# Starting the attention jobs 13 instead of 16 ticks behind the first feed-forward job, and the second feed-forward jobs 22 instead of 25

## The chip, the core and the metric

The kernel runs on one core of a Trainium2 chip. The metric is the device time of one execution, in microseconds (us). The core's engines are called PE (TensorE, matrix products and transposes), DVE (VectorE), ACT (ScalarE), POOL (GpSimd) and SP (SyncE, which issues the DMAs); each runs its own instructions in order and waits for the others by semaphores.

## What is computed

Sixteen sequences of 512 tokens with 128 channels go through four residual parts, all in fp32. `_L0_attn_a_ref` is an RWKV model of four layers (64 layer-and-sequence steps), `_L0_ffn_ref` a gated feed-forward with blockwise FP4 rounding of its inputs, `_L0_attn_b_ref` a causal attention with one head.

```python
    x = L0_attn_a_x
    x = x + _L0_attn_a_ref(_layernorm(x, axis=-1), ...)
    x = x + _L0_ffn_ref(_layernorm(x, axis=-1), L0_ffn_w_gate, L0_ffn_w_up, L0_ffn_w_down)
    x = x + _L0_attn_b_ref(_layernorm(x, axis=-1), L0_attn_b_w_qkv, L0_attn_b_w_out, L0_attn_b_b_out)
    x = x + _L0_ffn_ref(_layernorm(x, axis=-1), L0_ffn_w_gate, L0_ffn_w_up, L0_ffn_w_down)
    return x
```

## The kernel before

All sixteen sequences stay in SBUF as `X[0]` to `X[15]`, each 128 partitions by 512. The kernel is a software pipeline over **ticks**. Each engine has a loop `for t in range(TICKS)` (DVE L532, POOL L723, ACT L983, PE L1267) that calls the same small functions in a fixed order every tick; each call stands a fixed number of ticks behind the start of its job, and does nothing when no job is at that stage. Nothing in the program lets one tick wait for another: the engines drift against each other as far as the semaphores between them allow.

There are four kinds of jobs, one per sequence: the 64 RWKV steps (one per tick from tick 0), 16 first FFN jobs from tick `FFN_AT` = 69, 16 attention jobs from tick `ATT_AT` = 85, and 16 second FFN jobs from tick `FFN2_AT` = 94. `ffn_job(t)` and `att_job(t)` give the job that starts at tick t, or None.

An FFN job that starts at tick s occupies the engines so. DVE takes the statistics of the input, `f_bn` (two instructions of L225), at s-1. ACT normalises (`f_z`, four of L754) at s+2, keeps the turned input (`keep_fx`) at s+4, and takes silu of the four gate products (`silu`, L903) at s+5. PE turns the input (`f_turn`, L1037) at s+5, makes gate and up products (`f_gate` L1185 and `f_up` L1192) for token chunk 0 at s+5 and for chunks 1 to 3 at s+6, turns the quantised hidden values (`h_turn`, three groups of L1201) at s+8, and multiplies down (`down`, L1213) at s+9, after which ACT writes the new `X` (`keep_x`, L938).

An attention job that starts at tick s: statistics on DVE (`a_bn`, two of L225) at s+2, `a_rsqrt` on POOL at s+5, `a_z` on ACT (L754) at s+3, `a_turn` on PE (L1037) at s+4, `a_keys` (L1229) at s+5, `a_values` (L1237) and the four `similarity` products (L1245) at s+6 with `a_mask`, `a_max` on DVE and `a_exp` on ACT (L973), then `p_turn` (L1253), `keep_pt` (L980), `p_values` (L1263) and `a_add` (DVE L526) at s+7. The second FFN job of the same sequence takes its statistics at s+8.

PSUM has eight banks, and all of them are shared. `hand_over` fixes, in the order of PE's program, whom a bank's next writer waits for. Banks `bF0` and `bF1` carry the FFN's gate and up products of chunks 1 and 3 (`bG`, `bU`) and the attention's similarities 0, 1 and 3 (`bS`); `bR` and `bKV` carry the FFN's rounding (`pM`) and similarity 2 and `p_values`.

```python
        bX, pX, bG, pG, bU, pU = bK, pK, [bV, bF0], [pV, pF0], [bO, bF1], [pO, pF1]
        bS, pS, bY, pY = [bF0, bF1, bR, bF0], [pF0, pF1, pR, pF0], [bT, bO, bT, bO], [pT, pO, pT, pO]
```

ACT evaluates its functions from a table that holds one set at a time. Exp (of `a_exp`) and silu are in different sets, and the compiler puts an ACT_TABLE_LOAD wherever the set changes.

Of the kernel before, what the change touches and what calls it, by code (L numbers as in the profile page):

```python
# [31 lines left out]
FFN_AT = NR + 5  # L32
LN2_LAG = 6
EARLY = 10
ATT_AT, FFN2_AT = FFN_AT + 16, FFN_AT + 25
TICKS = FFN2_AT + 35


# [1340 lines left out]
```

## Time and profile before

| | |
|---|---|
| time, median of 3 runs | 1372.84 us (1369.95 to 1373.4) |
| span of the profiled execution, first to last instruction | 1368.5 us |
| PE busy | 1303.0 us (95%) |
| ACT busy | 1257.6 us (92%) |
| DVE busy | 1238.3 us (90%) |
| POOL busy | 1122.6 us (82%) |
| the 16 DMA engines | 4.2% for the data queue |

Busy time is the time in which an engine had at least one instruction in it. The profiled execution's own time is its span and what lies around it; the median of the runs stands 4.3 us above the span. PE's records are modelled at their ends, so a row of PE is best read by the distance from its start to the start of the next one.

### The profile page before, as it was taken

How to read it: one execution, taken by the hardware profiler on the slowest of the kernel's cores; microseconds unless marked ns; L12 is line 12 of the kernel's file. 1: busy time of each engine (PE TensorE's matmuls, PEld its weight loads, DVE VectorE, ACT ScalarE, POOL GpSimd, SP SyncE). 2: the span in 40 equal slices, each digit the busy share in tenths (PEclk: the TensorE clock that was granted, in tenths of full speed). 3: DMA queues.
4: the chain of work that ended last, by engine and by line, in shares of the span. 5: the costliest groups of instructions: out<-in, count | busy, mean ns of one | idle time of the engine just before them, and what ended most of it. 6: DMA issues, size and time to landing. Idle time of an engine off the chain costs nothing.

```text
span 1368.5 us, 23485 instructions
## 1 busy us (share of the span) xinstructions
PE 1303.0 (95%) x7285; PEld 935.9 (68%) x7285; DVE 1238.3 (90%) x2169; ACT 1257.6 (92%) x2539; POOL 1122.6 (82%) x1216
## 2 busy tenths in 40 slices
PE   3799999999999999999999999988999998899997
PEld 1356677667766677667766677766777876677776
DVE  6999999999999999999999999569999577978994
ACT  6899999999999999999999999877887899998884
POOL 6888998888888888888899999979998465666784
PEclk9899999999999999999999999999999999999999
DMA  7000000000000000000000000010000000000011
GB/s 237 1 1 1 1 1 1 1 21 13 1 0 2 1 1 1 1 1 1 1 1 1 8 24 21 27 32 1 1 1 1 2 1 1 1 16 16 24 32 39
DMA packets 26923, 18.54 MB, mean 14 GB/s; under 512 B 1072, under 2 KB 26160, under 8 KB 26800
## 3 DMA queue, kind: packets, MB, share of 16 engines
q1 hardware_dynamic: 26800, 17.05, 4.2%
q8 instruction: 59, 0.97, 0.3%
q14 instruction: 64, 0.52, 0.1%
HBM read 12.85 MB, written 4.19 MB: 12 GB/s over the span
## 4 chain that ended last, share of the span: by engine, by line
PE 67%; ACT 11%; DVE 9%; POOL 6%; issue 5%; DMA 0%; SPq 0%; DVEq 0%; ACTq 0%; POOLq 0%
PE ps L1154 12%; PE ps L1137 12%; PE ps L1213 5%; PE ps L1037 4%; PE ps L1192 4%; PE ps L1185 4%; PE ps L1144 3%; PE ps L1124 3%; PE ps L1089 3%; PE ps L1090 3%; PE ps L1102 3%; PE ps L1082 3%; PE ps L1263 3%; PE ps L1201 2%; PE ps L1245 2%
## 5 line engine op out<-in xcount | busy, mean ns | idle before, releaser
L1137 PE MATMUL ps<-xk,W 128*128 128x512 f32 x512 | 250.7, 593 | 1.4 <-ACT kf L864 1.4
L1154 PE MATMUL ps<-W,kf 128*128 128x128 f32 x2048 | 249.6, 275 | 0.0
L754 ACT ACTIVATE z<-X,ln_rs 128x128 f32<-128x128 f32 x512 | 239.7, 720 | 3.7 <-POOL ln_rs L603 3.7
L1154 PEld LDWEIGHTS ps<-W,kf 128*128 128x128 f32 x2048 | 239.2, 192 | 2.3 <-issue 1.0
L864 ACT ACTIVATE kf<-ps 128x512 f32<-128x512 f32 x256 | 186.6, 817 | 0.5 <-PE ps L1137 0.5
L871 ACT ACTIVATE kf<-kf 128x1024 f32<-128x1024 f32 x128 | 164.6, 1286 | 0.0
L1037 PEld LDWEIGHTS ps<-idn,z 128*128 128x128 f32 x664 | 83.1, 143 | 113.3 <-issue 87.3
L1137 PEld LDWEIGHTS ps<-xk,W 128*128 128x128 f32 x512 | 91.9, 190 | 92.1 <-issue 89.0
L710 POOL TENSOR_TENSOR W<-W,hsc 128x704 f32<-128x704 f32 x64 | 88.8, 1388 | 59.0 <-DVE W L493 58.8
L1037 PE MATMUL ps<-idn,z 128*128 128x128 f32 x664 | 102.0, 277 | 29.8 <-ACT z L754 20.7
L601 POOL TENSOR_TENSOR ln_rs<-ln_rs,mhalf 128x8 f32<-128x8 f32 (+1 forms) x70 | 127.9, 1827 | 0.0
L1185 PE MATMUL ps<-WG,d 128*128 128x352 f32 x256 | 98.5, 468 | 6.3 <-ACT er L903 5.4
L652 POOL TENSOR_TENSOR rv<-rv,aa 128x512 f32<-128x512 f32 x64 | 81.7, 1276 | 25.6 <-DVE aa L365 25.3
L670 POOL TENSOR_TENSOR dh<-h 128x512 f32<-128x512 f32 x64 | 66.5, 1039 | 43.3 <-ACT h L857 43.3
L225 DVE BATCH_NORM_STATS2 ln_st<-X 128x6 f32<-128x256 f32 x256 | 96.7, 419 | 0.1
L704 POOL TENSOR_TENSOR W<-W,hsc 128x704 f32<-128x704 f32 x64 | 88.8, 1389 | 8.6 <-DVE hsc L481 8.6
L1192 PE MATMUL ps<-WU,d 128*128 128x352 f32 x256 | 93.8, 466 | 1.9 <-DVE W L462 1.4
L1124 PEld LDWEIGHTS ps<-W,rc 128*128 128x128 f32 x512 | 68.0, 194 | 31.6 <-issue 29.0
L675 POOL TENSOR_TENSOR X<-X,cr 128x512 f32<-128x512 f32 x64 | 81.9, 1279 | 4.9 <-DVE cr L417 4.9
L657 POOL TENSOR_TENSOR er<-er,rc 128x512 f32<-128x512 f32 x64 | 81.6, 1276 | 0.0
L646 POOL TENSOR_TENSOR er<-er,bb 128x512 f32<-128x512 f32 x64 | 81.5, 1274 | 0.0
L663 POOL TENSOR_TENSOR p<-p,rc 128x512 f32<-128x512 f32 x64 | 81.5, 1273 | 0.0
(176 smaller groups left out, 3962.5 us busy)
## 6 DMA issues: line engine op xcount, KB each, us to landing
X<-x_in SPq DMA_DIRECT2D x16, 256.0 KB, 6.9
xi<-x_in SPq DMA_DIRECT2D x16, 256.0 KB, 2.9
out<-X SPq DMA_DIRECT2D x16, 256.0 KB, 2.3
W<-weights SPq DMA_DIRECT2D x4, 832.0 KB, 8.4
W<-fp4w SPq DMA_DIRECT2D x1, 560.0 KB, 3.8
row<-rows SPq DMA_DIRECT2D x1, 192.0 KB, 2.9
wqkv<-qkv SPq DMA_DIRECT2D x1, 96.0 KB, 5.7
idn<-ident SPq DMA_DIRECT2D x1, 64.0 KB, 3.1
```

Source lines behind the costliest of these rows:

```text
L225: last = e.bn_stats(g.of(g.st, n)[:, 2 * k:2 * k + 2, :].rearrange("p a s -> p (a s)"), src[:, k * 256:(k + 1) * 256].rearrange("p (a c) - ...
L601: e.tensor_tensor(rs[:, 0, :], rs[:, 2, :], mhalf[:, 0:k], ALU.pow).then_inc(*own.next())
L704: e.tensor_tensor(h, h, spread(hsc[n % 2][:, 0, k * 44:(k + 1) * 44], 44), ALU.mult).then_inc(fh_y[k], 1)
L754: last = e.activation(chunk(dst, j), chunk(src, j), ACT.Identity, bias=rs[:, 1, j:j + 1], scale=rs[:, 0, j:j + 1])
L864: e.activation(kf[r % 3][:, f, :], (pF0, pF1)[f % 2][:, :], ACT.Relu).then_inc(relu_done[f], 1)
L871: e.activation(both, both, ACT.Square).then_inc(sq_done[k], 1)
L1037: last = e.transpose(chunk(dst, j), chunk(src, j), idn[:, :])
L1124: last = e.matmul(chunk(pO, j), chunk(rc[r % 2], j), w_of(r, WO), start=True, stop=True)
L1137: e.matmul((pF0, pF1)[f % 2][:, :], w_of(r, WCK + f), xk[r % 2][:, :], start=True, stop=True).then_inc(kf_mm[f], 1)
L1154: last = e.matmul(chunk(pKV, j), kf[r % 3][:, f, j * 128:(j + 1) * 128], w_of(r, WCV + f), start=f == 0 and j == 0, stop=f == 3, skip_grou ...
L1185: e.matmul(pG[j % 2][:, 0:I], chunk(fx[n % 2], j), WG[:, :], start=True, stop=True).then_inc(g_mm, 1)
L1192: e.matmul(pU[j % 2][:, 0:I], chunk(fx[n % 2], j), WU[:, :], start=True, stop=True).then_inc(u_mm, 1)
```

## The change

Two numbers in one line: the first attention job starts at tick 82 instead of 85, the first job of the second FFN at tick 91 instead of 94. The distance between these two stays 9 ticks, the first FFN and the RWKV part keep their ticks. `TICKS` follows `FFN2_AT` and falls from 129 to 126.

```diff
 FFN_AT = NR + 5
 LN2_LAG = 6
 EARLY = 10
-ATT_AT, FFN2_AT = FFN_AT + 16, FFN_AT + 25
+ATT_AT, FFN2_AT = FFN_AT + 13, FFN_AT + 22
 TICKS = FFN2_AT + 35
```

The same compute instructions are issued, in another order on PE, DVE, ACT and POOL; SP's order is the same. ACT has 20 table loads before and 24 after.

On ACT, the place where the first attention job takes its exponentials (`a_exp`, L973, out `kf`), with the FFN's silu on L903 and its Abs on L916. Before:

```order
L938 ACTIVATE X<-ps 128x512
L973 ACT_TABLE_LOAD
L973 ACTIVATE kf,sm<-ps,sm 128x128
L965 ACTIVATE sr<-ps 128x512
L958 ACTIVATE ag<-ps 128x512
L973 ACTIVATE kf,sm<-ps,sm 128x256
L973 ACTIVATE kf,sm<-ps,sm 128x384
L952 ACTIVATE xc<-ps 128x512
L926 ACTIVATE W<-ps 96x512
L973 ACTIVATE kf,sm<-ps,sm 128x512
L933 ACTIVATE ps<-X 128x512
L754 ACTIVATE z<-X,at_rs 128x128 x4
```

And the same place in the program of the change:

```order
L973 ACT_TABLE_LOAD
L973 ACTIVATE kf,sm<-ps,sm 128x128
L965 ACTIVATE sr<-ps 128x512
L958 ACTIVATE ag<-ps 128x512
L973 ACTIVATE kf,sm<-ps,sm 128x256
L973 ACTIVATE kf,sm<-ps,sm 128x384
L952 ACTIVATE xc<-ps 128x512
L926 ACTIVATE ed<-ps 96x512
L973 ACTIVATE kf,sm<-ps,sm 128x512
L903 ACT_TABLE_LOAD
L903 ACTIVATE er<-ps 128x352
L916 ACTIVATE ps<-W 128x2x352
```

Before, the last silu of the first FFN lies behind ACT when the first exponential comes. Now the first attention job's exponentials stand between silus of the first FFN, so the table is loaded back behind them; this happens in two ticks (88 and 89), with two loads in each.

On PE, the place around the first attention job's `p_values` (L1263). Before, the tick held beside it only the last of the first FFN's turns and down products (L1201, L1213):

```order
L1245 MATMUL ps<-xc,ag 128x512
L1037 MATMUL ps<-idn,z 128x128 x4
L1201 MATMUL ps<-idn,W 96x128 x4
L1263 MATMUL ps<-sr,kf 128x128 x10
L1245 MATMUL ps<-xc,ag 128x128
L1213 MATMUL ps<-WD,ed 128x128 x12
L1253 MATMUL ps<-idn,big 128x128 x7
```

And now it stands among gate and up products (L1185, L1192) too:

```order
L1245 MATMUL ps<-xc,ag 128x512
L1037 MATMUL ps<-idn,z 128x128 x4
L1201 MATMUL ps<-idn,W 96x128 x4
L1192 MATMUL ps<-WU,d 128x352
L1263 MATMUL ps<-sr,kf 128x128 x10
L1185 MATMUL ps<-WG,d 128x352
L1192 MATMUL ps<-WU,d 128x352
L1185 MATMUL ps<-WG,d 128x352 x2
L1192 MATMUL ps<-WU,d 128x352 x2
L1201 MATMUL ps<-idn,W 128x128 x8
```

The job whose p_values stand there is the same; it is the FFN work around it that is of an earlier stage, by three ticks.

On DVE, the place where the first attention statistics (`a_bn`, at_st) come: in the program of the change they stand in a tick in which every stage of the first FFN on DVE but `f_bn` is still full.

```order
 L462 TENSOR_TENSOR W<-er,ps 128x352
 L255 TENSOR_REDUCE xsc<-z 128x32
+L225 BN_STATS at_st<-X 128x6 x2
 L446 SCALAR_TENSOR_TENSOR z<-ps,z 128x512
 L462 TENSOR_TENSOR W<-er,ps 128x352
```

Two instructions came into this tick (84), and into the next two; before, the first three of them stood in ticks 87 to 89.

## Rows read from the trace of the kernel before

**Rows 1.** The page: busy time of the engines, and slices of DVE and granted clock.

```profile
PE 1303.0 (95%) x7285; PEld 935.9 (68%) x7285; DVE 1238.3 (90%) x2169; ACT 1257.6 (92%) x2539; POOL 1122.6 (82%) x1216
...
DVE  6999999999999999999999999569999577978994
...
PEclk9899999999999999999999999999999999999999
```

**Rows 2.** Busy time by stretch, cut at PE's tick ends, ticks 84 to 98.

```profile
core 0: us, PE busy (x) PEld busy (x) DVE busy (x) ACT busy (x) POOL busy (x), PEclk, DMA share, GB/s
993.00:1002.90 9.90, 9.60 (x57) 7.16 (x56) 9.90 (x19) 8.15 (x18) 9.11 (x11) 1.00 0.01 2
1002.90:1039.80 36.90, 36.90 (x225) 28.86 (x224) 36.79 (x64) 30.61 (x62) 32.37 (x32) 1.00 0.00 1
1039.80:1049.40 9.60, 9.60 (x62) 7.76 (x61) 9.00 (x15) 8.00 (x18) 7.68 (x9) 1.00 0.00 1
1049.40:1059.20 9.80, 9.11 (x55) 6.85 (x53) 9.05 (x16) 7.20 (x16) 7.92 (x10) 1.00 0.00 0
1059.20:1069.10 9.90, 8.54 (x59) 6.98 (x58) 6.19 (x12) 9.60 (x22) 8.13 (x9) 1.00 0.01 2
1069.10:1082.00 12.90, 12.41 (x91) 10.54 (x90) 4.76 (x14) 11.15 (x30) 3.90 (x8) 1.00 0.01 2
1082.00:1092.40 10.40, 10.40 (x79) 8.98 (x78) 5.60 (x17) 7.68 (x22) 2.39 (x6) 1.00 0.00 0
1092.40:1131.80 39.40, 39.08 (x263) 31.03 (x262) 31.46 (x94) 37.36 (x108) 24.89 (x46) 1.00 0.01 1
```

**Rows 3.** PE's instructions in order of time, in tick 91: start, length, releaser.

```profile
1060.59 1.06 PE L1201 MATMUL ps<-idn,W 128*128 128x128 f32 x8 [1.36 <-POOL W L710]
1061.49 0.39 PE L1245 MATMUL ps<-xc,ag 128*128 128x128 f32 x2
1061.71 2.84 PE L1213 MATMUL ps<-WD,ed 128*128 128x128 f32 x24
1064.39 1.06 PE L1237 MATMUL ps<-AW,xc 128*128 128x128 f32 x8
...
1068.08 0.60 PE L1037 MATMUL ps<-idn,z 128*128 128x128 f32 x4
```

**Rows 4.** DVE's busy time in its ticks 83 and 84, and the attention's statistics.

```profile
993.10:1003.00 9.90, 9.90 (x20) 1.00 0.01 2
1003.00:1012.30 9.30, 9.30 (x18) 1.00 0.00 0
...
L225 DVE BATCH_NORM_STATS2 at_st<-X x32: 400/416/428, 1031.8 to 1191.0; 128x6 f32<-128x256 f32 x32
```

**Rows 5.** Busy time by stretch, as rows 2, in PE's ticks 99 and 103.

```profile
1131.80:1144.80 13.00, 10.02 (x61) 7.46 (x60) 8.89 (x23) 12.18 (x29) 6.71 (x12) 1.00 0.00 1
...
1191.70:1209.60 17.90, 17.40 (x110) 13.62 (x109) 14.24 (x31) 16.82 (x38) 11.98 (x16) 1.00 0.06 16
```

**Rows 6.** The chain of waits through tick 103: start, us, what.

```profile
1200.10 1.03 ACT h L754 x3
...
1202.11 0.87 ACT kf L980 x2
1203.00 1.28 ACT L973
1204.29 0.47 ACT kf L973 x2
1204.80 1.13 PE ps L1245 x2
...
1207.39 2.23 PE ps L1263 x20
1209.63 0.59 PE ps L1185 x2
...
1211.60 0.30 ACT er L903
```

**Rows 7.** ACT's writes of X behind the down products: min/median/max, first and last start.

```profile
L938 ACT ACTIVATE X<-ps x32: 574/591/612, 942.5 to 1365.6; 128x512 f32<-128x512 f32 x32
```

## The prediction

> **What bounds the kernel now.** I read the page's busy line first. PE is busy for 1303.0 of 1368.5 us, ACT 1257.6, DVE 1238.3 [rows 1]. Four engines lie so close that a mean over the kernel says nothing about one stage. The slices show where DVE dips (the 5, 6 and 7 behind the middle), and that the granted clock stays at its upper level apart from one slice [rows 1]; the stretch that the change touches runs at 1.00 throughout [rows 2]. So next I cut the stretch around the change into ticks. In the trace of PE a tick that holds only FFN work ends with an up product (L1192) and one with attention in it ends with `p_values` (L1263) or a turn, so the ends can be counted off from the order of the program. Ticks 84 to 98 run from 993.0 to 1131.8 us: 138.8 us [rows 2].
>
> What the reader is to see there is that PE alone sets these ticks. Ticks 85 to 88, with FFN work alone, take 36.9 / 4 = 9.2 us each and PE is busy for all of it, while DVE, ACT and POOL end below or at that. Ticks 94 to 98, with attention alone (and only the early DVE and ACT stages of the second FFN), take 39.4 / 5 = 7.9 us, again with PE busy for 39.08 [rows 2]. The lull between the two FFNs, which looks like free room in the schedule, is no lull on PE.
>
> **What the change does to PE's work.** From tick 96 on the changed program is, tick for tick, what the old one is from tick 99 on: attention and the second FFN keep their distance of 9, and the first FFN is over in both. What is left to compare is old ticks 84 to 98 (15 ticks) with new ticks 84 to 95 (12 ticks). The matrix products in them are the same ones. I call work the time that PE needs for them without waits.
>
> An FFN tick is 9.2 us. Its parts: eight gate and up products of 0.59 us [rows 6], the down group of 1061.71 to 1064.39, 2.7 us, a turn of 0.44, and three hidden turns of 0.45 (two of them in 1060.59 to 1061.49) [rows 3]. That makes 4.7 + 2.7 + 0.4 + 1.4 = 9.2, as measured. While the first FFN runs out, tick 90 has no input turn and no products of chunk 0 (9.2 - 1.6 = 7.6), ticks 91 and 92 have turns and down only (4.05 each), tick 93 down alone (2.7): 18.4 us.
>
> An attention tick is 7.7 us. I take that from tick 93, 10.4 us without an idle moment [rows 2], less 2.7 for down. While attention fills, its first tick adds a turn (0.45), the second keys too (1.3), the third values and similarities too: 0.2 from 1061.49, 3.7 from 1064.39 to 1068.08, and the turn of 0.45, 4.4 in all [rows 3].
>
> Old ticks 84 to 98: 6 x 9.2 + 18.4 for the FFN, 0.45 + 1.3 + 4.4 + 7 x 7.7 for attention, together 133.6 us. Measured are 138.8, so 5.2 us are waits or stretched work. By tick: 84 has 0.7 (9.9 against 9.2), 90 has 0.9 (9.8 against 8.9), 91 has 1.45 (9.9 against 8.45), 92 has 1.15 (12.9 against 11.75), 94 to 98 have 0.9 (39.4 against 38.5).
>
> New ticks 84 to 95, work by tick: 9.2, 9.2, 9.65, 10.5, 13.6, 16.9, 15.3, 11.75, 11.75, 10.4, 7.7, 7.7. The sum is the same 133.6 us. Three ticks are gone, but each of their microseconds stands in another tick. All that the change can win is out of the 5.2 us, and it can add waits of its own.
>
> **The waits of the new order, term by term.**
>
> Tick 84 keeps its 0.7 us, since it follows DVE's tick 83, which is not changed.
>
> DVE. With `f_bn` a DVE tick is 9.9 us, without it 9.3, and DVE is full in both; the attention's statistics are two instructions of 0.416 us, the same as those of the FFN [rows 4]. Old DVE ticks 84 to 86 had none; new ones have `a_bn`, so they stay at 9.9. PE follows one tick later, in ticks 85, 86 and 87, whose work is 9.2, 9.65 and 10.5: 0.7 + 0.25 + 0 = 0.95 us. The ends: nothing, if DVE has run ahead far enough, and 3 x 0.7 = 2.1 if PE feels all three. I take 0.95, since the full DVE in rows 4 leaves no lead to live on. Later DVE is no bound: its tick 89 would hold 14.2 at most, as the full one of rows 5, against 16.9 on PE.
>
> ACT. The chain of waits through tick 103, the first with all of attention and FFN in it, shows how such a tick closes: ACT works from the silu of chunk 1 to the table load and the first exponential (1204.29), PE does similarities, a turn and `p_values` (1207.39, 2.23 us), then the gate product of chunk 1, whose bank `bF0` the last exponential must have freed (1209.63), then comes the load back, and silu again at 1211.60 [rows 6]. That cycle is 17.9 us against 16.9 of work, 1.0 over [rows 5]. New tick 88 has the same loop without `f_z` (at least 1.03), without `keep_pt` (0.87) and without `p_values` (2.23) [rows 6]: 17.9 - 4.1 = 13.8 against PE's 13.6. New tick 89 has the loop without `f_z`, 16.9 against 16.9. I put 0.5 us on each, 1.0 together. The ends: nothing for both, and from above the price of tick 99, the first old tick in which silu meets exp: 13.0 us against 7.7 + 1.6 = 9.3 of work, 3.7 over [rows 5], plus the 1.0 of tick 103, 4.7 together. I stay near the lower end because tick 99 has little PE work and these two have 13.6 and 16.9. The price of the two ticks contains two table loads each, four more than before, each 1.28 us long [rows 6]. They are hidden by PE's work; bare, they would be 5.1 us.
>
> The Trainium skill bears on this price. Its page "ScalarE: Activation LUTs", in the section "What ACT_TABLE_LOAD costs", puts a switch of sets at 1283 ns for the load plus about 1380 ns for a drain. By that the four new loads would be 10.6 us of ACT instead of 5.1, and if the difference of 5.5 lay wholly on the path the change would end slower. The trace speaks against the second part: the copy before the load ends at 1202.98, the load starts at 1203.00 and the first exponential at 1204.29 [rows 6], so that one switch takes 1.29 us from end to start.
>
> The first FFN's end. Old ticks 90 to 92 lose 3.5 us because they are short: PE waits 1.36 us in tick 91 for the hidden values that POOL scales (L710, whose input comes by way of DVE) [rows 3]. In the new order the same steps have ticks of 15.3 and 11.75 us around them, longer than the chain they wait for. I take 0.8 us for ticks 90 to 93, between nothing and the old 3.5.
>
> Ticks 94 and 95 keep the 0.9 us of old 94 to 98, which lies at the entry to the second FFN and moves with it.
>
> POOL gets three more `a_rsqrt` into ticks where it is busy for 32.37 of 36.9 us [rows 2]; it stood at 9.11 in a tick of 9.9 with the FFN's own rsqrt in it, and the new POOL ticks 87 to 89 are of that make while PE's have 9.65 and more. Nothing. The DMAs keep their order and their data; the share is 0.01 or less here [rows 2]. Nothing.
>
> Sum: 0.7 + 0.95 + 1.0 + 0.8 + 0.9 = 4.35 us of waits instead of 5.2, so 0.8 us less, a span of 1367.7. The median of the runs stands 4.3 us above the profiled span, and the same difference gives **1372.0 us**. The ends add up to 0.7 + 0 + 0 + 0 + 0.9 = 1.6 (3.6 us less, 1369.2) and 0.7 + 2.1 + 4.7 + 3.5 + 0.9 = 11.9 (6.7 us more, 1379.5).
>
> **The rivals.** A first rival is that fewer ticks mean less time: three attention-only ticks of 7.7 us vanish into ticks in which other engines wait, 23 us, 1349.7. What would be for it is the dip of DVE [rows 1]. Against it: PE has no idle time in those ticks to give [rows 2]. Chance 3 in 100.
>
> A second is the forecast without new waits: the old stalls at the first FFN's end go and neither DVE nor ACT adds any. That is the lower end, 1369.2. For it speaks that the new ticks are long; against it the full DVE of rows 4. Chance 12 in 100, of which 3 lie beyond the 0.3%.
>
> The third ends on the other side. ACT sets the pace wherever silu and exp alternate, and PE's larger work does not hide it, because each needs the other's bank within the tick. The price is that of tick 99, 3.7 us, in tick 88, in 89 and again in 90, whose exponentials still follow the FFN's last stages: 11.1 instead of 1.0, 10.1 us more than forecast, 1382.1. It decides (over 0.3%) once ticks 88 to 90 have 5.9 us over their work. For it: old tick 99, and 17.9 in tick 103 with ACT busy for 16.82 [rows 5]. Against it: the loop of tick 88 counted above, 13.8. Chance 14 in 100. By the skill's drain it would be 5.5 us more than forecast with the loads alone, 1377.5, at 1 in 100, since the row shows no drain.
>
> The last is that the change does not do what it says, because attention waits for its input and starts no earlier. The first `X` of the first FFN is written at 942.5 us, one per tick follows [rows 7], and the first `a_bn` would come at about 1004 instead of 1031.8 [rows 4]; six ticks lie between, so I give it 2 in 100 (the time would stay within 0.3%).
>
> **How the numbers follow.** Forecast 68 in 100, the others as given (3, 12, 14, 1, 2). A difference of 0.3%, 4.1 us, is about what a measurement of this kernel can tell from none. Faster by more: 3 + 3 and 1 from the forecast's own tail, 0.07. Slower by more: 14 + 1 and 1 from the tail, 0.16. Within: 0.77. The range runs from the lower end, 1369.2, to 1379; beyond it lie the first rival, the beyond-0.3% part of the second and most of the third, under 2 in 10.
>
> **What would show it.** In the trace after, new ticks 84 to 95 should span 138 us or so beside 138.8 for old 84 to 98, and the part from tick 96 on should be as long as the old part from 99 on. PE's ticks 85 and 86 should take 9.9. Tick 88 should be 14 us and tick 89 between 17 and 17.5; if they are 17 and 20 with PE waiting for L903 or L973, the third rival is right. PE's wait for POOL L710 should be gone. I would be wrong altogether if the part behind tick 96 changed its length, for I count it as untouched.

## The result and the profile after

The change makes the kernel a little slower. Its median is 1376.97 us (1373.45 to 1378.29, 14 runs), that of the kernel before 1372.37 us (1369.83 to 1373.56, 14 runs); the ratio is 1.0030, 95% interval 1.0023 to 1.0038, so 3.2 to 5.2 us more. The forecast was 1372.0 us and no difference, with a range of 1369.2 to 1379 in which the measured time lies; slower by over 0.3% had a chance of 0.16, and the measured difference stands at the edge of that.

The page after has the same picture as [rows 1], with 4.2 us more on ACT, 4.1 more on PE, and DVE's dip between the FFNs partly filled:

```profile
PE 1307.1 (95%) x7285; PEld 937.6 (68%) x7285; DVE 1238.3 (90%) x2169; ACT 1261.8 (92%) x2543; POOL 1121.8 (82%) x1216
...
DVE  6999999999999999999999999569997767978994
```

ACT's four more instructions (2543 against 2539) are the table loads. The profiled span is 1375.7 us, 7.2 more than before. To see where that lies, both traces are cut at PE's tick ends, as in [rows 2]. Tick 83 ends at 993.0 us before and at 996.4 after; this step of 3.4 us, all but 0.5 of it in tick 74, is not of the change (see the last section). New ticks 84 to 95 take 142.5 us, where old 84 to 98 took 138.8. The rest takes 236.8 us after, 236.7 before. So the change costs 3.7 us, all of it in the twelve ticks in which the forecast had looked for it. The lowest times of the two kernels say the same: four lie at 1369.8 to 1370.0 before and three at 1373.5 after. The medians stand 4.6 us apart; how often the step in tick 74 occurs goes into them too.

Busy time of those ticks after, columns as in [rows 2] (ticks 84 to 93 one by one, then 94 and 95):

```profile
996.40:1006.30 9.90, 9.60 (x57) 7.17 (x56) 9.90 (x19) 8.15 (x18) 9.09 (x11) 1.00 0.01 2
1006.30:1016.10 9.80, 9.50 (x57) 7.09 (x56) 9.80 (x19) 8.05 (x18) 9.32 (x14) 1.00 0.00 0
1016.10:1026.80 10.70, 10.13 (x62) 7.78 (x61) 10.70 (x20) 9.29 (x22) 10.46 (x12) 1.00 0.01 2
1026.80:1038.80 12.00, 10.96 (x63) 8.08 (x62) 10.29 (x19) 10.30 (x22) 11.63 (x13) 1.00 0.00 1
1038.80:1052.30 13.50, 13.50 (x78) 9.98 (x77) 12.07 (x23) 12.36 (x28) 11.10 (x12) 1.00 0.01 2
1052.30:1070.90 18.60, 17.34 (x109) 13.84 (x110) 12.61 (x25) 15.91 (x36) 8.93 (x12) 1.00 0.00 1
1070.90:1087.10 16.20, 15.49 (x103) 12.40 (x102) 12.57 (x27) 14.13 (x31) 8.75 (x10) 1.00 0.01 2
1087.10:1100.70 13.60, 12.01 (x91) 10.33 (x90) 8.87 (x21) 11.08 (x28) 7.30 (x12) 1.00 0.00 0
1100.70:1112.40 11.70, 11.70 (x91) 10.28 (x88) 5.60 (x17) 9.14 (x25) 4.51 (x10) 1.00 0.01 3
1112.40:1122.80 10.40, 10.40 (x78) 8.98 (x78) 6.19 (x18) 9.17 (x26) 3.51 (x8) 1.00 0.01 2
1122.80:1138.90 16.10, 15.78 (x107) 12.25 (x106) 14.40 (x42) 16.10 (x47) 11.89 (x21) 1.00 0.00 0
```

The reader is to compare the first number of each row with the work that the prediction worked out for the tick: 9.2, 9.2, 9.65, 10.5, 13.6, 16.9, 15.3, 11.75, 11.75, 10.4 and 15.4. The cuts lie up to 0.1 us beside the ticks' ends; where they differ (ticks 85 and 86 are 9.9 and 10.6), the lengths of the next section are used. Tick 88 is at its work to 0.1 us, and 92 and 93 too. Over their work are 84 (0.7), 85 (0.7), 86 (0.95), 87 (1.5), 89 (1.7), 90 (0.9), 91 (1.85) and the last two (0.7). In tick 86 the row shows DVE at 10.70 of 10.70, POOL at 10.46 and ACT at 9.29; in tick 87 POOL stands at 11.63 of 12.00.

What PE waited for, in PE's instructions in order of time after, the waits in brackets (ticks 86, 87, 87, 89, 89, 90 and 91):

```profile
1018.92 0.86 PE L1185 MATMUL ps<-WG,d 128*128 128x352 f32 x2 [0.57 <-ACT er L903]
...
1028.28 0.86 PE L1185 MATMUL ps<-WG,d 128*128 128x352 f32 x2 [0.35 <-ACT ed L926]
...
1036.19 1.12 PE L1229 MATMUL ps<-xc,AW 128*128 128x512 f32 x2 [0.69 <-ACT X L938]
...
1053.29 0.86 PE L1185 MATMUL ps<-WG,d 128*128 128x352 f32 x2 [0.99 <-ACT kf L973]
...
1056.04 0.86 PE L1185 MATMUL ps<-WG,d 128*128 128x352 f32 x2 [0.27 <-ACT er L903]
...
1073.43 0.86 PE L1185 MATMUL ps<-WG,d 128*128 128x352 f32 x2 [0.71 <-ACT er L903]
...
1089.83 2.94 PE L1213 MATMUL ps<-WD,ed 128*128 128x128 f32 x24 [1.59 <-ACT ps L933]
```

PE's wait for POOL L710 [rows 3] is gone, as forecast. In its place stand seven short waits in ticks 86 to 91, all of them for ACT. Outside of these, PE waits 0.30 us for DVE in tick 84 (as before) and now also in tick 85, and 0.32 us for DVE in tick 95 (before in 98). The 0.69 us in front of the keys product (L1229) is an old one: in the kernel before it stood in tick 90.

### The profile page after: what moved, and what is told of

It reads as the page before. It is cut to its first block, busy times and chain, and to the rows that moved or that the text cites. A ratio compares the mean times of both kernels' runs of the same rounds, so it can differ in the third digit from the quotient of the medians.

```text
span 1375.7 us, 23487 instructions
## 1 busy us (share of the span) xinstructions
PE 1307.1 (95%) x7285; PEld 937.6 (68%) x7285; DVE 1238.3 (90%) x2169; ACT 1261.8 (92%) x2543; POOL 1121.8 (82%) x1216
## 4 chain that ended last, share of the span: by engine, by line
PE 66%; ACT 13%; DVE 9%; POOL 7%; issue 5%; DMA 0%; SPq 0%; ACTq 0%; DVEq 0%; POOLq 0%
PE ps L1154 12%; PE ps L1137 12%; PE ps L1213 5%; PE ps L1037 4%; PE ps L1192 3%; PE ps L1185 3%; PE ps L1144 3%; PE ps L1089 3%; PE ps L1090 3%; PE ps L1124 3%; PE ps L1102 3%; PE ps L1082 3%; PE ps L1263 3%; ACT z L754 2%; PE ps L1201 2%
## 5 line engine op out<-in xcount | busy, mean ns | idle before, releaser
L1137 PE MATMUL ps<-xk,W 128*128 128x512 f32 x512 | 252.5, 597 | 1.2 <-ACT kf L864 1.2
L1137 PEld LDWEIGHTS ps<-xk,W 128*128 128x128 f32 x512 | 92.4, 191 | 92.5 <-issue 89.8
L710 POOL TENSOR_TENSOR W<-W,hsc 128x704 f32<-128x704 f32 x64 | 88.8, 1388 | 70.8 <-DVE W L493 70.4
L1185 PE MATMUL ps<-WG,d 128*128 128x352 f32 x256 | 98.7, 468 | 8.9 <-ACT er L903 6.7
L1192 PE MATMUL ps<-WU,d 128*128 128x352 f32 x256 | 94.5, 468 | 2.2 <-DVE W L462 1.7
L1124 PEld LDWEIGHTS ps<-W,rc 128*128 128x128 f32 x512 | 67.9, 194 | 32.2 <-issue 29.2
```

The lines of the kernel that those rows point to most:

```text
L1124: last = e.matmul(chunk(pO, j), chunk(rc[r % 2], j), w_of(r, WO), start=True, stop=True)
L1137: e.matmul((pF0, pF1)[f % 2][:, :], w_of(r, WCK + f), xk[r % 2][:, :], start=True, stop=True).then_inc(kf_mm[f], 1)
L1185: e.matmul(pG[j % 2][:, 0:I], chunk(fx[n % 2], j), WG[:, :], start=True, stop=True).then_inc(g_mm, 1)
L1192: e.matmul(pU[j % 2][:, 0:I], chunk(fx[n % 2], j), WU[:, :], start=True, stop=True).then_inc(u_mm, 1)
```

## The experiments

Besides the times, each run gives the lengths of PE's ticks from its trace. In the stretch shown here they repeat to 0.1 us wherever the program is the same, which is what makes differences under 1 us readable. In the traces of the kernels below the lines of the functions behind an edit are shifted by a few. Comments in the diffs are added here. Lengths of PE's ticks in us, worked out from the traces:

```
tick            84    85    86    87    88    89    90    91    92    93
before         9.9   9.2   9.2   9.2   9.3   9.6   9.8   9.9  12.9  10.4
after          9.9   9.9  10.6  12.0  13.5  18.6  16.2  13.6  11.7  10.4
shift15        9.9   9.2   9.2   9.9   9.7  11.4  11.9  13.7  11.7  10.4
shift14        9.9   9.2   9.9  10.3  11.4  13.5  17.5  13.6  11.7  10.4
tanh_after     9.9   9.9  10.6  12.0  13.5  18.1  15.2  13.6  11.7  10.4
putx90         9.9   9.9  10.6  12.0  13.5  18.6  16.2  13.1  11.7  10.4
magic90        9.9   9.9  10.6  12.0  13.5  18.6  16.2  13.5  11.7  10.4
keys87         9.9   9.9  10.6  11.1  14.3  18.6  16.2  13.6  11.7  10.4
no_rsqrt15     9.9   9.9  10.3  12.0  13.5  18.6  16.2  13.6  11.7  10.4
no_bn          9.9   9.2  11.2  12.0  13.5  18.6  16.2  13.6  11.7  10.4
no_az          9.9   9.9  10.6  11.7  13.5  18.9  16.2  13.6  11.7  10.4
lean3          9.9   9.2   9.7  11.4  13.5  18.9  16.2  13.6  11.7  10.4
```

**How the cost grows with the shift.** Two kernels between the two, `shift15` and `shift14`:

```diff
-ATT_AT, FFN2_AT = FFN_AT + 16, FFN_AT + 25
+ATT_AT, FFN2_AT = FFN_AT + 15, FFN_AT + 24      # shift15
+ATT_AT, FFN2_AT = FFN_AT + 14, FFN_AT + 23      # shift14
```

> Attention 15 and second FFN 24 ticks behind the first FFN job, one tick earlier than before. Main theory (PE's work is conserved, and the 3.7 us that the change adds in ticks 84 to 95 are waits of single meetings, the largest where silu and exp alternate in ticks 88 and 89 and where the first FFN's end meets the attention's banks): the last silu is in tick 89 and the first exponential in tick 90, so no meeting; within 1 us of before. Rival (each tick less in the gap costs about a third of the 3.7 us, because PE has no idle time to give and every engine is fuller): +1.2 us. Table loads: 20, as before, so a rival of table loads alone says 0.

> Attention 14 and second FFN 23 ticks behind. One tick (89) has both silu and exp. Main theory: +1 to +2 us, and PE's waits for L903 or L973 appear in one tick. Rival of even cost per tick: +2.5 us. Table loads alone: two more, at most +2.6 us.

`shift15` ran at 0.9991 of before (0.9982 to 1.0000), `shift14` at 1.0024 (1.0013 to 1.0035). From tick 84 to the end of the trace the four kernels take 375.6 (before), 375.4, 378.0 and 379.3 us. The first tick of the shift is free, the second costs 2.6 us, the third 1.3. An even price per tick, the rival, does not fit the free first tick, though for `shift14` alone its 2.5 us were nearer than the 1 to 2 us of the main theory. In `shift14` silu and exp meet in one tick, and PE's waits for L973 and L903 appear at once, and the wait of the down group is at its full size:

```profile
1057.97 0.86 PE L1185 MATMUL ps<-WG,d 128*128 128x352 f32 x2 [0.99 <-ACT kf L973]
1060.72 0.86 PE L1185 MATMUL ps<-WG,d 128*128 128x352 f32 x2 [0.71 <-ACT er L903]
1077.12 2.95 PE L1213 MATMUL ps<-WD,ed 128*128 128x128 f32 x24 [1.59 <-ACT ps L933]
```

**The distance between attention and the second FFN.** In `att13_alone` only the attention moves, in `ffn2_28` only the second FFN, later; both have a distance of 12 instead of 9.

```diff
-ATT_AT, FFN2_AT = FFN_AT + 16, FFN_AT + 25
+ATT_AT, FFN2_AT = FFN_AT + 13, FFN_AT + 25      # att13_alone
+ATT_AT, FFN2_AT = FFN_AT + 16, FFN_AT + 28      # ffn2_28
```

> Attention 13 ticks behind as in the change, second FFN kept at 25: their distance grows from 9 to 12. Main theory: ticks 84 to about 95 carry the same waits as in the change (+3.7 us against before), and behind them three of the eight ticks in which the second FFN's silu meets exp are gone, each of which had 1.5 to 3.7 us over PE's work; together 1 to 5 us faster than before. Rival (the second FFN's distance does not matter, since PE's work is conserved there too): +3.7 us, slower like the change.

> Attention kept at 16, second FFN at 28 instead of 25: distance 12, three ticks more in all. Main theory: nothing changes up to tick 98, three meetings of silu and exp go; 5 to 8 us faster than before although it has three ticks more. Rival (more ticks with less in them leave PE idle while the second FFN fills alone): 3 to 8 us slower.

Both expectations for the gain missed. `att13_alone` is at 1.0020 of before (1.0010 to 1.0030), `ffn2_28` at 1.0005 (0.9996 to 1.0014). From tick 84 on they take 378.0 and 375.8 us. Ticks 84 to 93 of `att13_alone` are those of the change, which shows that the second FFN has no part in the 3.7 us. The three meetings that `ffn2_28` loses are ticks of 17.9, 17.9 and 16.9 us before, 52.7 together. In their place come three attention-only ticks of 7.7 or 7.8 and three FFN-only ticks of 9.9, 53 us together: the statistics of the second FFN, which lay beside long attention ticks, now make DVE the longest in ticks that hold FFN work alone (busy for 9.89 of 9.89 us in ticks 110 to 112, with PE waiting 0.29 us for it in each). One full engine was exchanged for another.

**The table loads.** `tanh_before` and `tanh_after` exchange the function, in the kernel before and in the changed one:

```diff
-                    e.activation(th[i % 2][:, 0:I], pG[j % 2][:, 0:I], ACT.Silu).then_inc(silu_done, 1)
+                    e.activation(th[i % 2][:, 0:I], pG[j % 2][:, 0:I], ACT.Tanh).then_inc(silu_done, 1)
```

> The kernel before with Tanh in place of Silu on ACT (the first FFN's and second FFN's gate then is a tanh, not a silu): Tanh and Exp are in one table set, so ACT's 20 table loads become 1, and nothing else changes. Theory of the exp and silu meeting: ticks 99 to 107, where each tick has two loads, lose 1 to 2 us each, 10 us or more in all. Theory that the loads lie beside PE's work: under 3 us.

> The changed kernel with the same exchange of Silu for Tanh. Theory that the table loads make most of the change's 3.7 us: against tanh_before it is less than 1.5 us longer behind tick 83, and ticks 89 and 90 have 17.0 and 15.4 us instead of 18.6 and 16.2. Rival (normalisations, banks and full engines, not the loads): it stays 3 us or more longer than tanh_before.

The medians are 1364.01 and 1364.79 us, 0.9937 (0.9924 to 0.9951) and 0.9944 (0.9931 to 0.9956) of before. Ticks 99 to 107 of `tanh_before` take 132.8 us where the kernel before has 143.6: the 16 loads in eight ticks of meeting cost 10.8 us, 0.7 each. Nothing else changes on ACT: a Tanh lasts 0.455 us in the mean and a Silu 0.458. Tick 103, which took 17.90 us with PE at 17.40 and ACT at 16.82 [rows 5], is then a tick of PE alone:

```profile
1195.10:1211.90 16.80, 16.80 (x110) 13.54 (x109) 14.06 (x32) 14.48 (x37) 10.26 (x12) 1.00 0.06 17
```

For the change it says this: `tanh_after` has 141.0 us in ticks 84 to 95, so 2.2 us more than the 138.8 that old 84 to 98 have with either function. Of the 3.7 us the four new loads are 1.5 (0.5 in tick 89, 1.0 in tick 90). The expected split (most of it loads) was wrong.

The page "ScalarE: Activation LUTs" of the Trainium skill (What ACT_TABLE_LOAD costs) gives 1283 ns for the load and 2.66 us per switch with its drain. The load lasts 1.28 us in the trace too, but no drain is seen behind it [rows 6], and on the path a load cost 0.7 us here.

**Ticks 85 to 88: one piece of work at a time.** Each of these kernels is the change with one piece taken out or moved. `no_bn` has a memset in place of `a_bn` for attention jobs 0 to 2, `no_rsqrt15` one small instruction in place of POOL's rsqrt for FFN job 15, `no_az` one activation in place of four in `a_z` of jobs 0 and 1. `keys87` moves the first keys product, which PE waits for, to the end of its tick.

```diff
 # no_bn
-                    stats(n_a, n, X[n])
+                    if n < 3:
+                        w.wait_ge(n_a.nr, n - 1)
+                        e.memset(n_a.of(n_a.st, n), 1.0).then_inc(n_a.stats, 1)
+                    else:
+                        stats(n_a, n, X[n])
 # no_rsqrt15
-                if n in range(2 * NB):
+                if n == NB - 1:
+                    w.wait_ge(n_f.z, n - 1)
+                    w.wait_ge(n_f.stats, n + 1)
+                    e.tensor_scalar(n_f.of(n_f.rs, n)[:, 1, :], n_f.of(n_f.st, n)[:, :, 1], -1.0, None,
+                                    ALU.mult).then_inc(n_f.nr, 1)
+                elif n in range(2 * NB):
 # no_az
-                    normalise(n_a, n, X[n], az[n % 2])
+                    if n < 2:
+                        w.wait_ge(n_a.nr, n + 1)
+                        rs = n_a.of(n_a.rs, n)
+                        e.activation(chunk(az[n % 2], 0), chunk(X[n], 0), ACT.Identity, bias=rs[:, 1, 0:1],
+                                     scale=rs[:, 0, 0:1]).then_inc(n_a.z, 1)
+                    else:
+                        normalise(n_a, n, X[n], az[n % 2])
 # keys87
-                a_keys(att_job(t - 5))
+                if t != 87:
+                    a_keys(att_job(t - 5))
...
                 f_up(ffn_job(t - 5), 0)
+                if t == 87:
+                    a_keys(att_job(t - 5))
```

> The change, with the attention's statistics of jobs 0 to 2 left out on DVE (a memset in their place; those sequences' normalisation is not computed). DVE rival: ticks 85 and 86 go back to 9.2 and 9.65, 1.6 us less. Main theory with POOL as the bound: about 0.7 us less in tick 85, and nothing in 86 and 87.

> The change, with the rsqrt of the first FFN's job 15 left out on POOL (one small instruction in its place; that sequence's normalisation is not computed). Main theory: in POOL ticks 86 and 87 the two rsqrts stand back to back, 3.5 us, which makes the rounding steps late for ACT and PE in ticks 86 and 87; PE's tick 86 goes from 10.6 to about 9.9 and 87 from 12.0 to about 11.3, in all 0.7 to 1.5 us less. Rival (DVE's statistics make these ticks long): no change.

> The change with three of the four activations of a_z left out for attention jobs 0 and 1 (their normalised input is then not computed but for one chunk). ACT has no idle moment there with both normalisations, 1.54 us each, in its ticks 85 and 86. If ACT is what makes PE's ticks 86 and 87 long: they go from 10.6 and 12.0 to about 9.9 and 11.3, 1.3 us less in all. If DVE or POOL is: no change.

> The change, with the attention's first keys product on PE moved, in tick 87 alone, from behind the down group to the tick's end. Main theory: PE's wait of 0.69 us for the copy of X out of the shared bank is filled with 1.5 us of turns and an up product, so tick 87 is 0.7 us shorter; ACT's next copy comes later, and up to 0.5 us may come back in tick 88. Rival (the 12.0 us of tick 87 are ACT being late from tick 86 on): no change over ticks 87 and 88 together.

Against before they ran at 1.0030 (1.0021 to 1.0040), 1.0024 (1.0014 to 1.0034), 1.0028 (1.0017 to 1.0038) and 1.0032 (1.0017 to 1.0046), which tells none of them from the change. The tick lengths do. Over ticks 85 to 87, which are 32.5 us in the change, `no_bn` has 32.5: its 0.7 in tick 85 comes back in tick 86. `no_rsqrt15` has 32.2. `no_az` has 32.1 and gives 0.3 back in tick 89. `keys87` shortens tick 87 by 0.9 and lengthens 88 by 0.8; its gate product now waits for ACT's copy, which came later because the keys did:

```profile
1039.84 0.86 PE L1185 MATMUL ps<-WG,d 128*128 128x352 f32 x2 [0.47 <-ACT W L926]
```

None of the four expectations came out as written. DVE alone as the cause would have given 1.6 us in `no_bn`, POOL alone at least 0.7 in `no_rsqrt15`, ACT alone 1.3 in `no_az`, and the keys product 0.7 in `keys87`, of which up to 0.5 could come back; they gave 0.0, 0.3, 0.4 and 0.1 to 0.2.

Who takes over from whom stands in ACT's instructions of tick 86. POOL works on the two rsqrts, that of FFN job 15 and that of attention job 0, from 1010.76 to 1014.42, one behind the other, and ACT waits for POOL's rounding steps behind them; PE's 0.57 us at 1018.92 are for the silu that stands between these two (after):

```profile
1017.89 0.60 ACT L909 ACTIVATE ps<-z 128x512 f32<-128x512 f32 x1 [1.04 <-POOL z L691]
1019.23 0.76 ACT L916 ACTIVATE ps<-W 128x704 f32<-128x704 f32 x1 [0.36 <-POOL W L704]
```

With DVE relieved (`no_bn`) the first of these waits grows to 1.69 us. With POOL relieved (`no_rsqrt15`) it is gone, and ACT waits for DVE a few instructions later, where it did not wait in the change:

```profile
1018.55 0.60 ACT L938 ACTIVATE ps<-X 128x512 f32<-128x512 f32 x1 [0.81 <-DVE z L452]
```

Behind that ACT, which does both normalisations in these ticks, has hardly an idle moment, as its instructions in the change from 1021.61 to 1029.65 show (start, length):

```profile
1021.61 1.64 ACT L754 ACTIVATE z<-X,at_rs 128x128 f32<-128x128 f32 x4
1023.15 0.59 ACT L926 ACTIVATE ed<-ps 128x512 f32<-128x512 f32 x1
1023.63 0.47 ACT L903 ACTIVATE er<-ps 128x352 f32<-128x352 f32 x1
1023.97 0.77 ACT L916 ACTIVATE ps<-W 128x704 f32<-128x704 f32 x1
1024.65 0.61 ACT L926 ACTIVATE ed<-ps 128x512 f32<-128x512 f32 x1
1025.13 1.65 ACT L754 ACTIVATE z<-X,ff_rs 128x128 f32<-128x128 f32 x4
1026.67 0.60 ACT L938 ACTIVATE X<-ps 128x512 f32<-128x512 f32 x1
```

**All three at once.** `lean3` holds the edits of `no_bn`, `no_rsqrt15` and `no_az` together; each begins so:

```diff
+                    if n < 3:                      # no_bn
...
+                if n == NB - 1:                    # no_rsqrt15
...
+                    if n < 2:                      # no_az
```

> The change with all three of the single pieces left out at once: the attention's statistics of jobs 0 to 2 on DVE, the rsqrt of the FFN's job 15 on POOL, and three of four activations of a_z of jobs 0 and 1 on ACT (these sequences are not normalised). Alone they were worth 0, 0.3 and 0.3 us. If ticks 85 to 87 are long because three engines are equally full there, and each takes over from the one relieved: together they give clearly more than 0.6, tick 85 goes to 9.2, 86 to about 9.7 and 87 to about 11.3, 2 us or more in all. Rival (one common cause that none of them touches): 0.6 us or less.

Its median is 1376.26 us, 1.0015 of before (1.0001 to 1.0030). Ticks 85, 86 and 87 are 9.2, 9.7 and 11.4 us as expected, 2.2 less than in the change, where the single edits had given 0.0, 0.3 and 0.4. It returns 0.3 us in tick 89, and 1.6 more near the end of the kernel (in ticks 108 and 113), so that the part behind tick 83 is 0.3 us shorter in all, 379.0 against 379.3. The one wait left in tick 87 is that for the shared bank (0.69). The three together are worth three times the sum of the single ones, so more than one engine holds these ticks. Whether two of the three edits would have done was not run.

**Tick 91: a bank handed on.** After the last exponential of tick 90 ACT stands still for 1.88 us in front of the Abs copy, and DVE's `a_add` ends just before it resumes:

```profile
1086.39 0.22 ACT L973 ACTIVATION_READ_ACCUMULATOR kf<-ps,sm 128x1 f32 x1
1088.49 0.76 ACT L916 ACTIVATE ps<-W 128x704 f32<-128x704 f32 x1 [1.88 <-issue]
1089.19 0.58 ACT L933 ACTIVATE ps<-X 128x512 f32<-128x512 f32 x1
...
1087.29 1.13 DVE L526 SCALAR_TENSOR_TENSOR X<-ps,sm,X 128x128 f32<-128x128 f32 x4 [1.45 <-PE ps L1263]
```

The bank `bKV` goes from `p_values` to `a_add` to the FFN's Abs copy, and the copy of X (L933), which needs no such bank, stands behind it, and PE's down group behind that. `putx90` and `magic90` change the order on ACT in tick 90 alone:

```diff
 # putx90
+                if t == 90:
+                    put_x(ffn_job(t - 8))
                 fh_magic(ffn_job(t - 6), 0)
 # magic90
-                fh_magic(ffn_job(t - 6), 0)
+                if t != 90:
+                    fh_magic(ffn_job(t - 6), 0)
...
                 keep_hq(ffn_job(t - 7), 0)
+                if t == 90:
+                    fh_magic(ffn_job(t - 6), 0)
```

> The change, but in tick 90 alone ACT copies X for the down product (put_x) ahead of the Abs copy (fh_magic), not behind it. Main theory: PE's wait of 1.59 us before the down group of tick 91 comes from p_values, a_add on DVE, the bank bKV that the Abs copy then gets, and the copy of X queued behind it; with the two exchanged that wait is gone, tick 91 goes from 13.6 to about 12.0 us and the part behind tick 83 from 379.3 to 377.7. Rival (PE waits there because ACT is behind as a whole): the wait moves by a few tenths at most.

> The change, but in ACT's tick 90 the Abs copy of job 15 (fh_magic), which waits 1.9 us for a_add to free the bank bKV, stands behind the copy of X, the normalisation and keep_hq, which need not wait. Theory of the bank: tick 91 goes from 13.6 to 12.0 us, and tick 92 stays. Rival (job 15's rounding is itself late then): tick 92 gets 0.5 to 1.5 us longer and takes it back.

They ran at 1.0024 (1.0012 to 1.0036) and 1.0025 (1.0015 to 1.0035) of before. PE's wait of 1.59 us is gone in both, so the chain was read rightly. But tick 91 gave only 0.5 us and less than 0.1, not 1.6. In `putx90` PE waits twice in the same tick for ACT's copies of the turned hidden values (L926), 0.44 and 0.50 us. In `magic90` PE waits a few instructions later for a copy that now stands behind the second half's Abs copy, which in turn waits for DVE to finish with the first half in the same bank:

```profile
1089.63 0.76 ACT L916 ACTIVATE ps<-W 128x704 f32<-128x704 f32 x1 [1.88 <-DVE W L493]
...
1090.96 0.55 PE L1256 MATMUL ps<-idn,kf 128*128 128x128 f32 x3 [1.64 <-ACT W L926]
```

So the bank is used by attention, first half and second half one after the other, and an exchange on ACT only chooses who stands behind it. How much a further bank would give was not tried, since all eight are in use.

**The weights turned in four ticks instead of one.** `weights_spread` is the kernel before with one piece of the FP4 weights' turning per tick on PE (72 to 75) and on ACT; the functions take the number of the piece:

```diff
-                if u == 0:
-                    weights_turned()
+                if -2 <= u < 1:
+                    weights_turned(u + 2)
+                if u == 1:
                     folded()
...
-                if u == 0:
-                    weights_kept()
+                if -2 <= u < 1:
+                    weights_kept(u + 2)
+                if u == 1:
                     folded_kept()
```

> The kernel before, with the turning of the FP4 weights spread on PE and ACT: one piece in each of ticks 72 to 75 instead of four pieces at once at the start of tick 74, where PE waits 0.98, 0.55 and 0.79 us for ACT's copies out of the one bank, and where the granted clock falls to 0.57 in some executions and not in others (905.3 or 908.8 us at the end of tick 74). If these waits are what the fall follows: PE's tick 74 is 2 to 5 us shorter, the two heaps of times of each kernel become one, and the median is 3 to 5 us below before. If the fall has another cause: the waits go (about 2 us), and the two heaps stay.

It is the fastest kernel here that computes all of the reference: 1369.21 us (1368.17 to 1371.3), 0.9978 of before (0.9969 to 0.9986), about 3 us less. Eight of its eleven times lie between 1368.2 and 1369.4 and three near 1371; of 21 times of the kernel before on the same chip, six lie at 1369.8 to 1370.3 and the others at 1371.9 or more. PE's tick 74 is 10.5 us instead of 14.2, as expected, but the two heaps of times did not become one.

## Why the prediction was wrong

It gave "no difference" 0.77 and forecast 0.8 us less; the change is 3.2 to 5.2 us slower. What was right is the frame. PE's work moved and did not shrink: the old and the new ticks have by its count the same 133.6 us of it, and the part from tick 96 on kept its length to 0.1 us. The first rival (three ticks less, 23 us) is refuted by that. The third (ACT sets ticks 88, 89 and 90, 11.1 us over their work) is refuted too: they have 2.5 over it together (-0.1, 1.7, 0.9). The input was there in time, as said: the first attention statistics start at 1008.1 us instead of 1031.8.

Of the signs set in advance, PE's wait for L710 is gone, the part behind tick 96 kept its length, and ticks 85 and 88 came as said (9.9 and 13.5 us). Ticks 84 to 95 took 142.5 us where 138 or so was said, tick 86 took 10.6 instead of 9.9, and tick 89 18.6 where 17 to 17.5 was said.

The step that failed is the sum of waits of the new order, 4.35 us forecast and 8.9 measured:

- **DVE, ticks 85 to 87: 0.95 forecast, 3.15 measured.** This is the largest miss. Tick 85 came as forecast (0.7, with PE waiting for DVE); ticks 86 and 87 have 0.95 and 1.5 where 0.25 and 0 were forecast. The prediction priced DVE alone, with "Nothing" for POOL, and did not price ACT there at all, although the stages of the jobs give ACT two normalisations in ticks 85 and 86. It had also read from rows 2 that PE alone sets the FFN ticks, where DVE is busy for 36.79 of the 36.9 us. In the trace after, POOL's two rsqrts make ACT wait 1.04 and 0.36 us and ACT's two normalisations keep it busy behind that; `no_bn`, `no_rsqrt15` and `no_az` show that relieving one engine gives at most 0.4, and `lean3` that relieving all three gives 2.2. The tick 87 term of 0 also forgot a wait that the prediction had counted in old tick 90: the keys product waits 0.69 us for ACT to empty the bank that it shares with the down group, and this moves with the attention. It was taken for a matter of short ticks.
- **ACT, ticks 88 and 89: 1.0 forecast, 1.6 measured.** The mechanism was right (the loop of exponential, bank, gate product and load), the size somewhat small: nothing in tick 88, where 0.5 was put, and 1.7 in tick 89. By `tanh_after`, 0.5 of it are the loads.
- **The first FFN's end, ticks 90 to 93: 0.8 forecast, 2.75 measured.** POOL's late step was covered, as forecast. But two others took its place: silu's load in tick 90 (1.0 by `tanh_after`), and in tick 91 the bank that goes from `a_add` to the Abs copy. The prediction counted the work of each engine per tick and not who holds a bank at the seam of two kinds of jobs. `putx90` shows 0.5 us of it to depend on ACT's order; the remaining 1.35 us in tick 91 are argued from the trace and not shown.
- **Ticks 94 and 95: 0.9 forecast, 0.7 measured; tick 84: 0.7 and 0.7.** Right.

The upper bounds set for the single terms (2.1, 4.7 and 3.5) held for all but the first, for which DVE alone gave too low a bound.

## What to carry to other kernels

When a software pipeline is packed tighter, first ask whether the longest engine has idle time in the ticks that vanish. If not, all that can be won is waits, and new ones can be added. Then write down for each new tick the work of every engine, not that of the fullest, and where several are nearly full expect the tick to be longer than any of them: tick 86 had 9.65 us of work on PE and took 10.6. List separately the buffers that two kinds of jobs hand to each other, since such a wait can move with the jobs, as the 0.69 us of the keys product did, and need not disappear in longer ticks. Where several engines are nearly full, do not expect much from relieving one; it gave at most 0.4 us here.

## What was not expected of the hardware

**A fall of the granted clock that comes in some executions only.** The step of 2.9 us ahead of the change lies in tick 74, which takes 14.2 us in the profile of before and 17.2 in that of after, with the same instructions. Busy time from 894 to 900 us in the two (before, then after), columns as in [rows 2]:

```profile
894.00:900.00 6.00, 5.21 (x30) 3.82 (x30) 2.44 (x6) 4.60 (x10) 5.45 (x9) 1.00 0.14 42
```

```profile
894.00:900.00 6.00, 5.21 (x12) 2.59 (x13) 1.49 (x4) 2.49 (x6) 4.92 (x8) 0.57 0.14 42
```

PE starts 12 instructions instead of 30 in the same 6 us, at a granted clock of 0.57 instead of 1.00, so mostly at the lower of its two levels. The four products of L1137 take 3.78 us there and 1.98 without the fall. In both, PE has just waited three times for ACT, here in the profile of after (PE in order of time):

```profile
892.88 0.52 PE L1045 MATMUL ps<-idn,W 128*128 128x128 f32 x3 [0.98 <-ACT WG L765]
893.96 0.55 PE L1049 MATMUL ps<-idn,W 128*128 128x128 f32 x3 [0.55 <-ACT WU L765]
895.29 0.77 PE L1055 MATMUL ps<-wqkv 64*128 64x128 f32 x2 [0.79 <-ACT WD L768]
...
896.41 3.78 PE L1137 MATMUL ps<-xk,W 128*128 128x512 f32 x4
```

Since the same three waits stand in the profile of before, they do not bring the fall by themselves. The times of most kernels here fall into heaps 2 to 3 us apart, as those listed for `weights_spread` and the kernel before do, and tick 74 takes 14.2, 15.8 or 17.0 to 17.3 us in the profiles. In `weights_spread` the three waits are gone (the longest wait of PE in ticks 73 and 74 is 0.43 us), its tick 74 is 10.5 us and most of its times are in the lower heap. Ticks 72 to 77 together are only 0.8 us shorter than those of the profile of before without the fall, and its lower heap stands about 1.2 us under that of before, so that most of the 3 us in the median is the fall avoided more often. That it is not avoided every time (3 of 11, judged from the times, since no trace of those three was kept) says that another cause is left, which was not looked for.

**Tick lengths repeat to 0.1 us.** From tick 80 on, kernels with the same program up to a tick have the same length of it to the tenth; where only an edited tick lies ahead, the later ones have it again, apart from one or two near the end. It does not hold everywhere: ticks 6 to 11 differ by up to 2.9 us between traces, tick 74 by 3.1 and tick 77 by 1.4. In ticks 84 to 95 differences of 0.3 us were readable from one trace each, a tenth of what the times of whole executions tell.

**Table loads cost less than they last.** 16 loads of 1.28 us in eight ticks cost 10.8 us, 0.7 each, and the four new ones of the change 1.5, 0.4 each (`tanh_before` and `tanh_after`).
